# Experts and mixture of a transformer megakernel as one unrolled instruction stream, with a gate per pair of sequences

## The chip, the cores and the metric

The kernel runs on one core of a Trainium2 chip. The metric is the time on the device in microseconds (us), the median of several executions. The engines are named as in the profile: PE is TensorE, PEld its weight load, DVE is VectorE, ACT is ScalarE, POOL is GpSimd, SP is SyncE, which issues most DMAs.

## The reference, cut to what matters

Sixteen sequences of 128 tokens and 128 features go through two transformer layers. Everything before the last two steps is left as it is by the change, apart from the places named below. The last two steps are these (`_L1_cond2_ref`, then `x = x + _L1_ffn_ref(x)`):

```python
s0, s1, s2 = (_dense(x, share_wi[i], share_wo[i]) for i in range(3))   # relu(x @ wi) @ wo, hidden width 512
out_a = relu(x @ expert_wi[type_idx]) @ expert_wo[type_idx]            # one of 3 types per sequence
out_b = relu(x @ expert_wi[type_idx + 1]) @ expert_wo[type_idx + 1]
p = softmax(gate_vecs / 0.1); wa, wb = p[type, type], p[type, type + 1]
expert_out = out_a * wa + out_b * wb
gi = concatenate([expert_out[:, 0], s0[:, 0], s1[:, 0], s2[:, 0]])     # the first token alone
g = softmax(relu(gi @ gate_w1) @ gate_w2)                              # 4 numbers per sequence
x = expert_out * g[0] + s0 * g[1] + s1 * g[2] + s2 * g[3]
# mixture: every token goes to one of 8 small networks (128 -> 128 -> 128)
idx = argmax(softmax(x @ Wg + bg))
x = x + (gelu(x @ W1[idx] + b1[idx]) @ W2[idx] + b2[idx])
```

## The kernel before

Features lie on the partitions and tokens along the free axis: `XT` is 128 x 2048 (16 sequences of 128 columns), `ZT` a second such tensor. Each engine has its own program, written out by hand and ordered by semaphores; there is no scheduler. The kernel runs in stages: a causal attention, a rigid transform of images, six layers of local attention with a feed-forward part (`pe_local`, `dve_local`, `act_local`, unrolled on every engine, the last slots being the drain of the last feed-forward chunk), a gated linear attention (GLA, a loop `Fori` over 4 chunks of 4 sequences), then what the change touches.

**Gate.** `gate_pe`, `gate_dve`, `gate_act` work out the gate for all 16 sequences before the experts start. The gate needs the first token's output of every expert, so `gate_pe` multiplies the 16 first columns (`first`) by all seven experts' up weights (L1682: 28 matmuls, each two records in the trace) and down weights (L1689, 28 more), then by `gate_w1` (L1694) and `gate_w2` (L1698). `gate_dve` also works out the type weights wa and wb (L1717 to L1741), and `scale5`, five factors per sequence, at the end. A float32 matmul is two records, a transpose one.

**Experts.** `Fori(0, B // 2)` runs over pairs of sequences, ten jobs a pair, five a sequence (two chosen experts, three shared). A job n is `up`: four matmuls 128 x 128 x 128 into a bank (L1788), a relu with the gate's factor (job even: ACT, L1827; job odd: DVE, L1824), and `down`: four matmuls (L1800), which accumulate all five jobs of a sequence in one 128 x 128 area of PSUM. PE's order is up(n+1), down(n). `experts_pe` starts every pair afresh with up(0). When a sequence is done, DVE copies it to `ZT` (L1831). POOL copies the two chosen experts' weights next to each other (`e_sel`, L1843 and L1844), two sequences ahead at most.

**Mixture.** `Fori(0, NCH)` runs over 4 chunks of 512 tokens. In each, DVE copies the chunk to `m_src` (L1888), PE computes the routing logits (L1853), DVE turns them into a one-hot matrix in six small ordered steps (L1890 to L1901), PE transposes it (L1858), DVE copies it out twice (L1904, L1905). Then PE starts with the biases `m_b2` (L1862) and goes through eight experts: up (L1867) and a matmul that spreads the one-hot row over the partitions (L1868), ACT Gelu (L1918), DVE product (L1908), PE down (L1875). DVE adds the result to `XT` (L1911). All of a chunk comes after all of the one before.

**Output.** When all four chunks are done, PE transposes `XT` in four groups (L1969), DVE copies each to `ZT` (L2032) and SP stores 1 MB in one DMA (L613).

Of the kernel before, what the change touches and what calls it, by code (L numbers as in the profile page):

```python
# [60 lines left out]
E_FREE, E_DOWN = 2, 10  # L61
ME = 8

# [48 lines left out]
class Semaphores:  # L112


    def __init__(self, sem):
# [91 lines left out]
        self.e_first = sem("e_first")  # L207
        self.e_gate_made = sem("e_gate_made")
        self.e_gate_read = sem("e_gate_read")
        self.e_steps = sem("e_steps")  # L210
        self.e_arg = sem("e_arg")
        self.e_exp = sem("e_exp")
        self.e_scales = sem("e_scales")
# [5 lines left out]
        self.e_scaled = sem("e_scaled")  # L219
        self.m_loaded = sem("m_loaded")  # L220
        self.m_copied = sem("m_copied")
# [47 lines left out]
def build(nc, d, out):  # L269
    with ExitStack() as ctx:  # L270
# [145 lines left out]
        first = sb("first", [P, B])  # L416
        gate_h = xf[0][:, 0:NEXP * FJ * B]
        gate_in, gate_hid = sb("gate_in", [P, 4 * B]), sb("gate_hid", [P, B])
        gate_p, gate_max, gate_diag = sb("gate_p", [B, 4]), sb("gate_max", [B, 1]), sb("gate_diag", [B, 4 * B])
# [3 lines left out]
        pick, expw = sb("pick", [P, 4 * B]), sb("expw", [P, 4 * B])  # L423
        scale5 = sb("scale5", [P, B, 5])
        e_scale = [sb(f"e_scale{i}", [P, 5]) for i in range(2)]
        e_h = t1
        m_w1, m_w2 = wv, wo[:, :, :].rearrange("p c e -> p (c e)")
        m_pick = sb("m_pick", [ME, ME * P], BF16)
        m_b2 = sb("m_b2", [ME, P])
        m_hotT, m_hot16 = qkT[0][0:ME, :], sb("m_hot16", [ME, CW], BF16)  # L430
        m_gate, m_gate_b, m_rank = sb("m_gate", [P, ME]), sb("m_gate_b", [P, ME]), sb("m_rank", [P, ME])
        m_logits, m_hot, m_max = sb("m_logits", [P, CH * ME]), sb("m_hot", [P, CH * ME]), sb("m_max", [P, CH])
        m_src, m_g, m_h = sq[0], t2, qn
# [23 lines left out]
        def live(t):  # L457
            return 0 <= t < LOCAL

        @block.sync  # L460
        def _(sp):
# [69 lines left out]
            sp.wait_ge(s.consts_set, 4)  # L531
# [34 lines left out]
            sp.dma_start(m_b2[:, :], d["L1_ffn_b2"]).then_inc(s.m_loaded, 16)  # L566
# [3 lines left out]
            for t in range(LOCAL + 32):  # L570
# [41 lines left out]
            sp.wait_ge(s.out_ready, 4)  # L612
            sp.dma_start(out.rearrange("b t f -> t b f"), ZT[:, :].rearrange("p (b f) -> p b f", b=B))\  # L613
                .then_inc(s.out_stored, 16)
            sp.wait_ge(s.out_stored, 16)

# [438 lines left out]

        def pe_local(pe):  # L1060
# [153 lines left out]
        def dve_local(dve):  # L1214
# [58 lines left out]
            dve.wait_ge(s.consts_set, 4)  # L1273
            tables(0)
            for u in range(SLOTS):
# [68 lines left out]
                if u % TICKS == TICKS // 2 and u // TICKS + 1 < DEPTH:  # L1344
                    tables(u // TICKS + 1)
                t = u - L_SCORE
# [9 lines left out]
        def act_local(act):  # L1356
# [23 lines left out]
            for u in range(SLOTS):  # L1380
# [36 lines left out]
                if live(t) and not bursts(u):  # L1417
                    act.wait_ge(a.qkT_ready, TICKS + t + 1)
                    act.wait_ge(a.sc_ready, TICKS + t - 1)
                    act.copy(qkT[t % 2][:, :], turn_ps[:, :]).then_inc(a.qkT_moved, 1)  # L1420
                if live(u) and u % GROUPS == 0:
# [254 lines left out]
        def gate_pe(pe):  # L1676
            pe.wait_ge(s.e_loaded, 16 * 9)
            pe.wait_ge(s.e_first, 1)
            for e in range(NEXP):
                for j in range(FJ):  # L1680
                    at = (e * FJ + j) * B
                    mm = pe.matmul(bank[0][:, at:at + B], up_of(e)[:, j * P:(j + 1) * P], first[:, :],  # L1682
                                   start=True, stop=True)
            mm.then_inc(s.e_gate_made, 1)
            pe.wait_ge(s.e_gate_read, 1)
            for e in range(NEXP):
                for j in range(FJ):
                    at = (e * FJ + j) * B
                    mm = pe.matmul(bank[1][:, e * B:(e + 1) * B], down_of(e)[:, j, :], gate_h[:, at:at + B],  # L1689
                                   start=(j == 0), stop=(j == FJ - 1))  # L1690
            mm.then_inc(s.e_gate_made, 1)
            pe.wait_ge(s.e_gate_read, 3)
            for k in range(4):
                mm = pe.matmul(bank[2][:, 0:B], gw1[:, k, :], gate_in[:, k * B:(k + 1) * B], start=(k == 0),  # L1694
                               stop=(k == 3))
# [434 lines left out]
```

## Time and profile before

| | us |
|---|---|
| median of three runs (2888.82 to 2893.68) | 2891.81 |
| the profiled execution's own time | 2897.6 |
| its span in the trace | 2894.8 |
| PE busy in the span | 2542.0 (88%) |
| DVE busy | 2098.2 (72%) |
| ACT busy | 1895.1 (65%) |
| mean granted TensorE clock | 0.949 |

The span is one execution as the profiler recorded it; 2.8 us of its time lie outside the span. "Granted clock" is the share of TensorE's full clock that the chip let through: 1.00 is 2.4 GHz, 0.50 is 1.2 GHz. Times that begin with a position (2604.37) count from the start of the span.

### The profile page before, as it was taken

How to read it: one execution, taken by the hardware profiler on the slowest of the kernel's cores; microseconds unless marked ns; L12 is line 12 of the kernel's file. 1: busy time of each engine (PE TensorE's matmuls, PEld its weight loads, DVE VectorE, ACT ScalarE, POOL GpSimd, SP SyncE). 2: the span in 40 equal slices, each digit the busy share in tenths (PEclk: the TensorE clock that was granted, in tenths of full speed). 3: DMA queues.
4: the chain of work that ended last, by engine and by line, in shares of the span. 5: the costliest groups of instructions: out<-in, count | busy, mean ns of one | idle time of the engine just before them, and what ended most of it. 6: DMA issues, size and time to landing. Idle time of an engine off the chain costs nothing.

```text
span 2894.8 us, 99523 instructions
## 1 busy us (share of the span) xinstructions
PE 2542.0 (88%) x36565; PEld 1731.7 (60%) x36565; DVE 2098.2 (72%) x4476; ACT 1895.1 (65%) x6628; POOL 1778.7 (61%) x1601
## 2 busy tenths in 40 slices
PE   6999787789999999999999999999999955569987
PEld 4566544456666666666666666666666623259932
DVE  6777799978888888888888888888888734432222
ACT  3666788867888788877888888877878722221121
POOL 1666787578777777777777777777777701002100
PEclk9999999999999999999999999999999966669987
DMA  4000100021112111211121111111111100000000
GB/s 128 10 11 11 45 13 13 11 77 34 32 40 54 38 33 40 53 39 32 39 54 39 32 43 50 40 32 44 49 39 32 32 19 0 0 0 0 0 0 14
DMA packets 177362, 92.10 MB, mean 32 GB/s; under 512 B 40902, under 2 KB 173208, under 8 KB 176928
## 3 DMA queue, kind: packets, MB, share of 16 engines
q1 hardware_dynamic: 168304, 82.00, 11.0%
q0 software_dynamic: 8192, 4.21, 1.1%
q8 instruction: 276, 4.52, 0.7%
q14 instruction: 158, 1.29, 0.1%
q10 hardware_dynamic: 432, 0.07, 0.0%
HBM read 32.06 MB, written 3.76 MB: 12 GB/s over the span
## 4 chain that ended last, share of the span: by engine, by line
POOL 32%; issue 19%; PE 17%; DVE 6%; ACT 3%; DMA 1%; SPq 1%; DVEq 0%; POOLq 0%; ACTq 0%; PEld 0%; PEldq 0%
POOL rs L1463 15%; POOL t_pair L1453 11%; POOL pr L1444 5%; PE bank L1800 2%; PE bank L1788 2%; PE bank L1084 1%; PE bank L1867 1%; PE scores L1129 1%; PE bank L1140 1%; DMA rg_prod<-vt 1%; PE scores L1875 1%; PE bank L1077 1%; PE bank L1169 1%; PE scores L1111 1%; ACT pr L1392 1%
## 5 line engine op out<-in xcount | busy, mean ns | idle before, releaser
L1463 POOL TENSOR_TENSOR rs<-ssc,neg_half 128x8 f32<-128x8 f32 x384 | 645.4, 1681 | 30.1 <-DVE ssc L1343 30.1
L1453 POOL TENSOR_TENSOR t_pair<-qn_pair,tabs 128x512 f32<-128x512 f32 x384 | 489.0, 1273 | 11.4 <-DVE qn_pair L1327 9.1
L1392 ACT ACTIVATE pr<-scores,negmax 128x64 f32<-128x64 f32 x1536 | 463.4, 319 | 3.8
L1444 POOL TENSOR_TENSOR pr<-pr,rec 128x256 f32<-128x256 f32 x384 | 235.7, 614 | 340.7 <-DVE rec L1320 340.7
L1077 PE MATMUL bank<-wqk,xs 128*128 128x512 f32 x768 | 396.8, 599 | 4.7 <-DVE qn_pair L1327 3.6
L1392 ACT ACTIVATION_READ_ACCUMULATOR pr<-scores,negmax 128x1 f32 x1536 | 321.5, 209 | 0.0
L1386 ACT COPY vt<-bank 128x256 f32<-128x256 f32 x361 | 134.5, 373 | 284.9 <-PE bank L1140 244.5
L1012 POOL DMA_INDIRECT rg_win<-rg_images,share_down x256 | 260.5, 1018 | 83.3 <-issue 55.8
L1084 PEld LDWEIGHTS bank<-ident,qr_pair 128*128 128x128 f32 x1536 | 180.2, 142 | 180.3 <-DVE qr_pair L1309 141.4
L1327 DVE TENSOR_TENSOR qn_pair<-bank,rs 128x512 f32<-128x512 f32 x384 | 260.4, 678 | 19.1 <-POOL rs L1463 19.1
L1309 DVE TENSOR_TENSOR qr_pair<-t_pair 128x512 f32<-128x512 f32 x384 | 264.7, 689 | 10.0
L1140 PE MATMUL bank<-wv,xs 128*128 128x256 f32 x768 | 269.5, 433 | 0.0
L1295 DVE TENSOR_TENSOR t_pair<-qn_pair,tabc 128x512 f32<-128x512 f32 x384 | 267.6, 697 | 0.0
L1084 PE MATMUL bank<-ident,qr_pair 128*128 128x128 f32 x1536 | 238.7, 278 | 29.0 <-DVE qr_pair L1309 26.0
L1339 DVE TENSOR_REDUCE ss<-sq 128x8 f32<-128x512 f32 x384 | 261.4, 681 | 2.9 <-ACT sq L1410 2.9
L1420 ACT COPY qkT<-bank 128x512 f32<-128x512 f32 x361 | 217.4, 602 | 58.2 <-PE bank L1084 54.8
L1352 DVE TENSOR_REDUCE negmax<-scores 128x4 f32<-128x256 f32 x384 | 162.9, 424 | 124.0 <-PE scores L1129 123.6
L1410 ACT ACTIVATE sq<-bank 128x512 f32<-128x512 f32 x384 | 244.2, 636 | 8.5 <-PE bank L1077 8.4
L1094 PEld LDWEIGHTS bank<-oT,wo 128*128 128x128 f32 x1536 | 232.6, 192 | 20.5 <-issue 0.5
L1094 PE MATMUL bank<-oT,wo 128*128 128x128 f32 x1536 | 234.6, 275 | 0.0
L1066 PEld LDWEIGHTS bank<-ident,pr 128*128 128x128 f32 x768 | 108.5, 142 | 201.7 <-issue 199.4
L1129 PE MATMUL scores<-pT,vt 64*64 64x64 f32 (+1 forms) x3072 | 211.9, 231 | 10.9 <-issue 5.6
(315 smaller groups left out, 5607.6 us busy)
## 6 DMA issues: line engine op xcount, KB each, us to landing
rg_prod<-vt SPq DMA_DIRECT2D x1536, 32.0 KB
wqk<-in_L_ffn_Wqkv SPq DMA_DIRECT2D x20, 256.0 KB, 3.1
rg_win<-rg_images,share_down POOLq DMA_INDIRECT x256, 2.4
wv<-in_L_ffn_Wqkv SPq DMA_DIRECT2D x20, 128.0 KB, 2.7
wo<-in_L_ffn_Wo SPq DMA_DIRECT2D x20, 128.0 KB
w<-in_L_ffn_W SPq DMA_DIRECT2D x6, 341.0 KB
rg_images<-rg_prod SPq DMA_DIRECT2D x1, 1625.0 KB, 8.4
rg_images<-XT SPq DMA_DIRECT2D x16, 64.0 KB, 1.5
```

Source lines behind the costliest of these rows:

```text
L1012: pool.indirect_dma_start(rg_win[:, b, g, :], None, rg_images.unsqueeze(1), bass.IndirectOffsetOnAxis(rg_index[:, n:n + 1], 0)).then_inc(s ...
L1077: pe.matmul(qk_ps[t % 2][:, :], xs[b % 2][:, :], wqk[:, g, :, :].rearrange("p i n -> p (i n)"), start=True, stop=True).then_inc(a.qk_ready, 1)
L1084: mm = pe.transpose(turn_ps[:, c * P:(c + 1) * P], qr[t % 2][:, c * P:(c + 1) * P], ident[:, :])
L1094: mm = pe.matmul(yl_ps, wo[:, 2 * g + c, :], oT[b % 2][:, (2 * g + c) * P:(2 * g + c + 1) * P], start=(g == 0 and c == 0), stop=(g == GROU ...
L1140: pe.matmul(vl_ps, xs[b % 2][:, :], wv[:, g * GV:(g + 1) * GV], start=True, stop=True)\
L1295: dve.tensor_tensor(t1[t % 2][:, :].rearrange("p (i h e) -> p i h e", i=2, h=GH), qn[t % 2][:, :].rearrange("p (i h e) -> p i h e", i=2, h ...
L1309: dve.tensor_tensor(qr[t % 2][:, :], t1[t % 2][:, :], t2[t % 2][:, :], ALU.add)\
L1339: dve.tensor_reduce(ss[t % 2][:, :, 0], heads(sq[t % 2][:, :]), AX.X, ALU.add).then_inc(a.summed, 1)
L1392: ex = act.activation(pr[t % 2][:, h * BAND:(h + 1) * BAND], sl_ps[:, h // 2, h % 2 * BAND:(h % 2 + 1) * BAND], ACT.Exp, bias=negmax[t % 2 ...
L1444: pool.tensor_tensor(p, p, over(rec[t % 2][:, :], [P, GH, BAND], 2), ALU.mult).then_inc(a.p_scaled, 1)
L1453: pool.tensor_tensor(t2[t % 2][:, :].rearrange("p (i h f e) -> p i h f e", i=2, h=GH, f=2), qn[t % 2][:, :].rearrange("p (i h f e) -> p i ...
L1463: pool.tensor_tensor(rs[t % 2][:, :], ssc[t % 2][:, :], neg_half[:, 0:8], ALU.pow)\
```

## The change

1. *Gate.* The separate gate stage is gone. Instead the experts keep their outputs apart: `down` writes the two chosen experts (scaled by wa and wb in the relu) to columns 0 to 127 of a bank and each shared expert to columns of its own. One bank (2 to 5) belongs to one sequence. From the first column of each of the four parts the gate of a pair is worked out within the stream of jobs: DVE copies (`first_token`), PE multiplies (`hidden`, `logits`), DVE and ACT form the softmax (`logits`, `soften`), and DVE mixes the four parts with the four factors into `ZT` (`combine`: four operations of 128 x 128 a sequence). This happens 10 to 17 jobs after the pair's first job.
2. *Type weights.* wa and wb (`types_dve`, 14 small operations with an Exp on ACT in the middle) move to the drain of the local stage, slot `LOCAL + L_PROJ + 2`.
3. *One stream.* Experts and mixture are unrolled: 80 jobs, then 32 (`MJOBS`). Routing of chunk 0 goes inside the experts (jobs 60 to 65), that of chunk c+1 inside chunk c. `m_src` is gone, PE reads `ZT`.
4. *Selection.* POOL prepares the first two sequences' weights before GLA.
5. *Output.* Each chunk is transposed one chunk later inside the stream (`turn_out`), copied by ACT (`leave`) and stored with a DMA of its own (256 KB).
6. *Padding.* `m_pick`, `m_b2`, `m_hotT`, `m_hot16` get 128 rows instead of 8, zeroed by POOL at the start, after the local stage and after GLA.

```diff
+        def experts_pe(pe):
+            def up(n):
+                b, x = divmod(n, 5)
+                if x == 0:
+                    pe.wait_ge(s.e_chosen, 2 * b + 2)
+                if n >= 2:
+                    pe.wait_ge(s.e_relu, n - 1)
...
+            def down(n):
+                b, x = divmod(n, 5)
+                pe.wait_ge(s.e_relu, n + 1)
+                if x == 0 and b >= 4:
+                    pe.wait_ge(s.e_moved, b - 3)
...
+                part = max(x - 1, 0) * P
+                for j in range(FJ):
+                    mm = pe.matmul(bank[2 + b % 4][:, part:part + P], w[:, j, :], e_h[n % 2][:, j * P:(j + 1) * P],
+                                   start=(x != 1 and j == 0), stop=(x != 0 and j == FJ - 1))
...
+            def hidden(i):
+                pe.wait_ge(s.e_gate_read, 4 * i + 2)
+                for k in range(4):
+                    mm = pe.matmul(hid_ps, gw1[:, k, :], gate_in[:, k, :], start=(k == 0), stop=(k == 3))
+            def logits(i):
+                pe.wait_ge(s.e_gate_read, 4 * i + 3)
+                for u in range(2):
+                    mm = pe.matmul(logit_ps[:, 4 * u:4 * u + 4], gate_hid[:, u:u + 1].to_broadcast([P, P]), gw2[:, :],
...
+            up(0)
+            for n in range(JOBS):
+                if n + 1 < JOBS:
+                    up(n + 1)
+                down(n)
+                i, step = gate_at(n)
+                if step == 2:
+                    hidden(i)
+                if step == 4:
+                    logits(i)
+                if n == M_FIRST:
+                    moe_logits(pe, 0)
+                if n == M_FIRST + 4:
+                    moe_turn(pe, 0)
+            pe.wait_ge(s.m_loaded, 16 * 6)
+            hidden(PAIRS - 1)
+            moe_up(pe, 0)
+            logits(PAIRS - 1)
...
+            def combine(i):
+                dve.wait_ge(s.e_exp, i + 2)
+                ordered(dve.tensor_reduce(gate_max[:, :], gate_p[:, :, :], AX.X, ALU.add))
+                ordered(dve.reciprocal(gate_max[:, :], gate_max[:, :]))
+                ordered(dve.tensor_tensor(gate_p[:, :, :], gate_p[:, :, :], over(gate_max[:, :], [P, 2, 4], 2), ALU.mult))
+                for k in range(4):
+                    for u in range(2):
+                        b = 2 * i + u
+                        to, part, by = ZT[:, b * P:(b + 1) * P], bank[2 + b % 4][:, k * P:(k + 1) * P], gate_p[:, u, k:k + 1]
+                        if k:
+                            dve.wait_ge(s.e_mixed, 6 * i + 2 * k - 1 + u)
+                            mix = dve.scalar_tensor_tensor(to, part, by, to, ALU.mult, ALU.add)
+                        else:
+                            mix = dve.tensor_scalar(to, part, by, None, ALU.mult)
...
+            for n in range(1, JOBS, 2):
+                relu_dve(dve, n)
+                if n % 10 == 7:
+                    first_token(2 * (n // 10))
+                i, step = gate_at(n)
+                if step == 1:
+                    first_token(2 * i + 1)
+                if step == 3:
+                    hidden(i)
+                if step == 5:
+                    logits(i)
+                if step == 7:
+                    combine(i)
+                if n == M_FIRST + 1:
+                    moe_choose(dve, 0)
+                if n == M_FIRST + 5:
+                    moe_hot(dve, 0)
+            first_token(B - 1)
+            hidden(PAIRS - 1)
+            logits(PAIRS - 1)
+            combine(PAIRS - 1)
...
+            for k in range(MJOBS):
+                c, e = divmod(k, ME)
+                if k + 1 < MJOBS:
+                    moe_up(pe, k + 1)
+                down(k)
+                if e == 1 and c + 1 < NCH:
+                    moe_logits(pe, c + 1)
+                if e == 5 and c + 1 < NCH:
+                    moe_turn(pe, c + 1)
+                if e == 3 and c:
+                    turn_out(c - 1)
+            turn_out(NCH - 1)
...
+            for c in range(NCH):
+                sp.wait_ge(s.out_ready, c + 1)
+                sp.dma_start(out[CH * c:CH * (c + 1)].rearrange("b t f -> t b f"),
+                             ZT[:, c * CW:(c + 1) * CW].rearrange("p (b f) -> p b f", b=CH)).then_inc(s.out_stored, 16)
...
+                if u == LOCAL + L_PROJ + 2:
+                    act.wait_ge(s.e_arg, 1)
+                    act.activation(typew[:, :], typew[:, :], ACT.Exp).then_inc(s.e_exp, 1)
...
+            pool.wait_ge(s.e_loaded, 16 * 9)
+            for b in range(2):
+                choose(pool, b)
             with pool.Fori(0, NCH) as c:
                 gla_pool(pool, c)
```

Here `gate_at(n)` gives pair `i = (n - 10) // 10` and step `(n - 10) % 10`.

## Rows read from the trace of the kernel before

**Rows 1.** The page: the span, and POOL's busy tenths in 40 slices.

```profile
span 2894.8 us, 99523 instructions
POOL 1666787578777777777777777777777701002100
```

**Rows 2.** Busy time by stage: window, length, then PE, PEld, DVE, ACT, POOL, clock.

```profile
2573.49:2604.37 30.88, 24.44 (x124) 23.88 (x125) 7.45 (x37) 1.14 (x3) 2.28 (x3) 0.55 0.00 1
2617.38:2636.86 19.48, 18.65 (x161) 18.09 (x161) 4.65 (x9) 3.44 (x5) 4.05 (x4) 1.00 0.00 1
...
2761.65:2792.50 30.85, 26.58 (x54) 8.72 (x54) 8.63 (x18) 6.78 (x9) 0.00 (x0) 0.78 0.00 1
...
2884.95:2894.80 9.85, 2.34 (x16) 1.69 (x16) 3.26 (x5) 0.00 (x0) 0.00 (x0) 0.80 0.38 106
```

**Rows 3.** Timeline of the gate stage: start, length, engine, what, idle before.

```profile
2573.79 0.16 DVE L1717 TENSOR_REDUCE typem<-typew 128x3 f32<-128x12 f32 x1
...
2574.02 4.40 PE L1682 MATMUL bank<-first,e_up_w 128*128 128x16 f32 x32 [1.26 <-DVE first L1712]
...
2574.45 0.21 ACT L1771 ACTIVATE typew<-typew 128x12 f32<-128x12 f32 x1 [0.23 <-DVEq L1720]
...
2604.37 3.56 PE L1788 MATMUL bank<-XT,rg_win 128*128 x16 [2.49 <-POOL rg_win L1844]
```

**Rows 4.** Timeline of the experts, the break in a pair and one job.

```profile
2635.60 0.29 DVE L1831 COPY ZT<-bank 128x128 f32 x1 [3.64 <-PE bank L1800]
...
2636.86 1.15 PE L1800 MATMUL bank<-t_pair,rg_win 128*128 128x128 f32 x8 [0.51 <-DVE t_pair L1824]
...
2637.85 1.06 PE L1788 MATMUL bank<-XT,bqk 128*128 x8
...
2639.12 0.75 DVE L1824 TENSOR_SCALAR t_pair<-bank,e_scale 128x512 f32<-128x512 f32 x1 [2.39 <-PE bank L1788]
...
2640.53 1.06 PE L1800 MATMUL bank<-t_pair,share_down 128*128 128x128 f32 x8
```

**Rows 5.** Timeline of the mixture's first chunk: routing, then two experts.

```profile
2762.68 1.06 PE L1853 MATMUL bank<-m_gate,sq 128*128 128x8 f32 x8 [1.15 <-DVE sq L1888]
...
2765.14 1.02 PE L1858 MATMUL bank<-ident,m_hot 128*8 128x128 f32 x4 [1.40 <-DVE m_hot L1901]
...
2779.45 0.69 DVE L1908 TENSOR_TENSOR qn_pair<-t_pair,bank 128x512 f32<-128x512 f32 x1 [3.33 <-ACT t_pair L1918]
...
2780.86 1.12 PE L1875 MATMUL scores<-qn_pair,wo 128*128 128x512 f32 x2
...
2781.82 1.02 PE L1867 MATMUL bank<-sq,wv 128*128 128x512 f32 x2
...
2783.09 1.12 PE L1875 MATMUL scores<-qn_pair,wo 128*128 128x512 f32 x2
```

**Rows 6.** Windows of 3 us around the start of the mixture.

```profile
2764.00:2767.00 3.00, 1.02 (x4) 0.35 (x4) 1.75 (x7) 0.00 (x0) 0.00 (x0) 0.60 0.01 3
...
2776.00:2779.00 3.00, 3.00 (x5) 0.72 (x4) 0.12 (x1) 0.27 (x1) 0.00 (x0) 0.63 0.00 0
```

**Rows 7.** Local stage: a group, busy and mean ns; then timeline of POOL and DVE.

```profile
L1303 DVE TENSOR_TENSOR ZT<-bank,ZT 128x128 f32<-128x128 f32 x12 | 3.4, 285 | 0.0
...
2102.09 1.63 POOL L1463 TENSOR_TENSOR rs<-ssc,neg_half 128x8 f32<-128x8 f32 x1
...
2103.01 0.68 DVE L1295 TENSOR_TENSOR t_pair<-qn_pair,tabc 128x512 f32<-128x512 f32 x1
```

**Rows 8.** Timeline of the drain of the local stage, the last chunk's Square.

```profile
2330.29 0.63 ACT L1373 ACTIVATE rg_prod<-rg_prod 128x512 f32<-128x512 f32 x1 [2.03 <-DVE rg_prod L1234]
```

**Rows 9.** Timeline of the output; then the page's DMA issues (last number: us to landing).

```profile
2886.51 1.29 DVE L2032 COPY ZT<-bank 128x512 f32<-128x512 f32 x2 [0.82 <-PE bank L1969]
...
2889.27 0.39 SPq L613 DMA_DIRECT2D out<-ZT  x1
...
wqk<-in_L_ffn_Wqkv SPq DMA_DIRECT2D x20, 256.0 KB, 3.1
```

More of the change, by code:

```diff
@@ L1671, in gla_pool @@
                 pool.tensor_tensor(grs[j % 2][:, :], gss[j % 2][:, :], neg_half[:, 0:GLH], ALU.pow).then_inc(s.g_rms, 1)
-        def gate_pe(pe):
-            pe.wait_ge(s.e_loaded, 16 * 9)
[L1678 to L1695, printed above, removed]
-            mm.then_inc(s.e_gate_made, 1)
-            pe.wait_ge(s.e_gate_read, 4)
-            pe.matmul(bank[3][0:B, 0:4], gate_hid[:, :], gw2[:, :], start=True, stop=True).then_inc(s.e_gate_made, 1)
-            pe.wait_ge(s.e_gate_read, 5)
-            pe.matmul(bank[4][:, 0:4 * B], ones[0:B, :], gate_diag[:, :], start=True, stop=True)\
-                .then_inc(s.e_gate_made, 1)
@@ new lines, in moe_hot, with moe_dve, masked, added @@
+            dve.tensor_copy(m_hot16[c % 2][0:ME, :], spot_of(c)[0:ME, :]).then_inc(s.m_hot, 1)
+        def moe_dve(dve):
+            def masked(k):
+                dve.wait_ge(s.m_gelu, k + 1)
+                if k >= 2:
+                    dve.wait_ge(s.m_up, k + 1)
+                dve.tensor_tensor(m_h[k % 2][:, :], m_g[k % 2][:, :], bank[2 + k % 2][:, :], ALU.mult)\
+                    .then_inc(s.m_masked, 1)
+            def added(c):
+                dve.wait_ge(s.m_y, c + 1)
+                dve.tensor_tensor(XT[:, chunk(c)], XT[:, chunk(c)], y_of(c), ALU.add).then_inc(s.m_added, 1)
+            for k in range(MJOBS):
+                c, e = divmod(k, ME)
+                masked(k)
+                if e == 0 and c:
+                    added(c - 1)
+                if e == 2 and c + 1 < NCH:
+                    moe_choose(dve, c + 1)
+                if e == 6 and c + 1 < NCH:
+                    moe_hot(dve, c + 1)
+            added(NCH - 1)
@@ L1919, in moe_act, with leave @@
+        def moe_act(act):
+            def leave(c):
+                act.wait_ge(s.out_turned, c + 1)
+                act.copy(ZT[:, chunk(c)], bank[4][:, :]).then_inc(s.out_ready, 1)
+            for k in range(MJOBS):
+                c, e = divmod(k, ME)
+                act.wait_ge(s.m_up, k + 1)
+                if k >= 2:
+                    act.wait_ge(s.m_masked, k - 1)
+                act.activation(m_g[k % 2][:, :], bank[k % 2][:, :], ACT.Gelu,
                                bias=cols[:, R_MB1 + e:R_MB1 + e + 1]).then_inc(s.m_gelu, 1)
+                if e == 5 and c:
+                    leave(c - 1)
+            leave(NCH - 1)
```

398 lines of the change are left out of this document (178 added, 220 removed).

## The prediction

> **What bounds the kernel now.** I read the page first, then busy time by stage, then the chain and the timeline of the last 320 us. The span is 2894.8 us [rows 1]; the change touches what lies behind 2573.49, and little before it. The reader is to see four kinds of time there.
>
> The gate stage lasts 30.9 us, from the end of GLA to the experts' first matmul at 2604.37 [rows 2, 3]. PE is busy in 24.4 of them, but with matmuls of 16 columns that mostly load weights, at a clock of 0.55.
>
> The experts run from 2604.37 to 2761.65, 157.3 us. A pair takes 19.48 us at clock 1.00 [rows 2]. Inside it 24 records, from the start of an up at 2637.85 to that of a down at 2640.53, take 2.68 us [rows 4]: 0.1117 us a record, 1.787 us a job, 17.87 us for ten. A pair loses 1.61 us where the pipeline breaks. The reader sees one break: DVE first copies the finished sequence to `ZT` (2635.60), its relu comes late, and PE waits for it until 2636.86.
>
> The mixture takes 30.85 us a chunk, 123.3 us up to 2884.95, at a mean clock of 0.78 [rows 2]. In the steady part an expert takes 2.23 us (2780.86 to 2783.09), PE without a gap [rows 5]; eight are 17.8 us. The other 13 us are routing, in which PE mostly waits for DVE, and the half clock that follows: 0.60 at 2764 to 2767, and still only 0.63 at 2776 to 2779 [rows 6], after PE had little but small matmuls and waits.
>
> The output takes 9.85 us [rows 2].
>
> **The change, part by part.**
>
> *Gate stage.* It goes as a whole. PE's first up needs `XT` and the selected weights; POOL makes these before GLA. DVE's first operation after GLA begins at 2573.79, PE's at 2574.02 with the copy of `first` between them [rows 3]. I let PE begin at 2573.8: 2604.37 - 2573.8 = **30.6 us less**. Both start with the clock in an unknown level; before, 16 records took 3.56 us, 0.22 each, so 1.7 us were lost there [rows 3]. I count the same loss after; none would be the lower bound.
>
> *Experts.* Unrolled, the eight breaks of 1.61 go: -12.9. PE gains `hidden`, 4 matmuls or 8 records a pair, and `logits`, 2 or 4 records. Tiny matmuls cost the weight load: 8 records of 8 columns took 1.06 with their drain [rows 5], the pitch is again about 0.11. So 12 x 0.1117 = 1.35 a pair, and 7 pairs in the stream: +9.4. Routing of chunk 0 adds 8 records, 0.9, and four transposes, whose records I take at 0.12: 0.5. Together -12.9 + 9.4 + 1.4 = **-2.1**.
>
> DVE's new work is hidden only if its relus stay in time, so it has to be costed. A relu starts 0.38 after the end of its up's stream (2637.85 + 8 x 0.1117 = 2638.74, to 2639.12) and lasts 0.75; its down starts at 2640.53, so it may come 0.6 late [rows 4]. DVE has one relu in two jobs, every 3.57 us. The fullest interval is that with `combine`: relu 0.75, `first_token` 0.17, three ordered small operations, eight mixes. Small ordered operations follow each other by 0.22 (three of them between 2573.79 and Exp at 2574.45) [rows 3]: 0.66. A mix is an operation on 128 x 128 with one input in PSUM; the nearest rows are 0.285 (an addition) and 0.29 (a copy) [rows 4, 7]. The wait in it is for the mix two before, of the other sequence's neighbour, which is done. I take 0.27 to 0.30 each: 2.3. Sum 3.9, so the next relu is 0.3 late, inside its slack of 0.6: nothing. Not covered, with 0.4 a mix, the interval is 4.8 and 0.6 a pair is lost, 4 us. In the intervals with `moe_choose` (six ordered steps, 1.35) and `moe_hot` the sum stays below 3.6.
>
> Behind `combine` wait ACT's next relu (by `e_relu`) and the down of the sequence four later (by `e_moved`), three jobs away. A PE head-of-line wait for `e_gate_read` finds DVE done two jobs earlier. ACT's Exp of 0.2 is small beside its idle time: ACT is busy 3.44 of 19.48 [rows 2].
>
> *Seam.* The last pair's gate is not hidden. From the end of the last down, T: `first_token` 0.2, `hidden` starts at T + 0.26 and ends at 1.3, DVE relu to 1.5; PE meanwhile does the mixture's first up and spread (1.27) to 2.5, `logits` to 2.95, then up 1 and the biases to 5.2. DVE's maximum and subtraction end at 3.5, Exp at 3.8, `combine` at 6.65, the first product (0.69 [rows 5]) at 7.35, PE goes on at 7.4. PE is thus idle or at the gate for 1.2 + 0.45 + 2.2 = 3.9 us. ACT's Gelu, which also needs another table, is ready at 5.7, before DVE.
>
> *Mixture.* 32 experts x 2.23 = 71.4. Biases 4 x 0.96 (a down alone takes 2780.86 to 2781.82 [rows 5]) = 3.8. Inside: three routings' logits 3 x 0.9 = 2.7, three transposes 1.5, three output transposes 1.5. Sum 80.9, with the seam 84.8. For a spell of half clock after the seam I add 1: the gap is 2.2 us where the old one had six with hardly any work, and 5 is the other bound (ten microseconds at half level, as after 2767 [rows 6]). 85.8 against 123.3: **-37.5**. DVE's product may be 0.7 late by the same reading (gelu, product, then down). Routing puts 0.69 + 1.35 before the next product, in a pitch of 2.23 that PE's 0.9 of logits widens: covered. If it isn't, 1 us for each of the three chunks is lost. Addition and `leave` fall where one operation of 0.7 has room.
>
> *Output.* Before, the first copy starts 1.56 after 2884.95; then 2.7 us for the rest of the copies, and 5.5 from the issue at 2889.27 to the end [rows 2, 9]. After: 1.56, one copy 0.65, one DMA of 256 KB, which lands in 3.1 [rows 9], plus 0.4 at the end: 5.7. **-4.2**; bounds -3 and -6.
>
> *Type weights in the drain.* DVE has room there, but ACT's Exp is put before the last chunk's Square, which started at 2330.29, at once when DVE was done [rows 8]. Exp can start 0.66 after DVE begins at about 2330.3 and takes 0.21 [rows 3]: Square waits until 2331.2, **+0.9**, on the chain of the drain. DVE's rest is done before the variance arrives. Bounds 0 and 2.
>
> *POOL.* Four copies of about 1 us move to the local stage's end, where POOL waits. The memsets at the start lie in a slice with POOL busy a tenth [rows 1]: nothing; uncovered a microsecond. The padding to 128 rows doesn't change the columns that a matmul streams: nothing, and no row prices it otherwise.
>
> *A rule that speaks against it.* In rows 7 a DVE operation with two SBUF inputs starts at 2103.01, in the middle of a POOL operation of 1.63 us on SBUF that began at 2102.09, and takes its usual 0.68. By the Trainium skill (SBUF — State Buffer, "Who interferes with whom") such a pair of operations shares a port as an exclusive lock, and the later one fully blocks. This row doesn't agree. By that rule the sum would be as in rival 2.
>
> **Sum.** 0.9 - 30.6 - 2.1 - 37.5 - 4.2 = -73.5 us. The profiled execution, 2894.8 of span and 2.8 around it, was 5.8 us above the median, which is 0.2%; the difference carries over: 2891.8 - 73.5 = **2818 us**, 2.5% less.
>
> **The rivals.**
>
> 1. *The forecast, 0.66.* Own range 2812 to 2826.
> 2. *POOL's weight copies block `combine`, 0.06.* They start after job 5b - 9, for every second sequence beside `combine`. The gate's multiplication has two SBUF inputs; waiting for a copy of 1 us would make the interval 4.9, 0.7 beyond the slack, 5 us over seven pairs, and 1 in the drain: 2824. Rows 7 speak against it.
> 3. *DVE becomes the bound, 0.12.* Each mix costs 0.45 for waits between neighbours, and routing misses its room: combine interval 5.2, 1.0 a pair lost, 7 us; 3 in the mixture: 2828, up to 2840 with 0.6 a mix. For it speaks that ordered steps show 0.06 of wait each; against it, that mixes alternate between two sequences.
> 4. *Half clock inside the stream, 0.08.* The clock falls at the seam and at some gates. A microsecond of dense work costs one more at half level. At the seam 5 instead of 1, and 2 for each of three gates: 2828 to 2835. For: small matmuls lay before the fall [rows 6]. Against: 1.35 us of them stand in 19 dense ones.
> 5. *Slower, 0.03.* The same mechanism without recovery: the stream would have some 235 us of dense work, and all at half clock gives 3050. It is slower than before from 73 us of such work on, a third of the stream. The experts stayed at 1.00 with PE waiting 1.6 us in a pair [rows 2], so it is unlikely.
> 6. *More gain, 0.05.* No half clock at the start and seam, Exp hidden, shorter store: 2812 or less.
>
> The Trainium skill (TensorE: Matmul & The Clock Gate, "HAM oscillation — how this bites in real kernels") says that bursts with gaps between them fall back to the slow clock each time; by that the seam alone would cost rival 4's 5 us. Rows 6 show it for the old routing; none shows it for a gap of two microseconds.
>
> **How the numbers follow.** Cases 1, 2, 3, 4 lie between 2812 and 2840, which holds a good 8 in 10: I give **2812 to 2842**. A measurement of this kernel can tell 0.2%, some 6 us, from no change. Faster by more than that: all but case 5 and a hundredth for mixtures of mishaps, 0.96; same 0.01; slower 0.03.
>
> **What the profile after would show.** PE's first `up` about 0.3 us after GLA's last addition, at clock 1.00 soon after. A pitch of 19.2 us per pair, with no PE wait for a DVE relu after `combine`; if DVE is the bound, these waits stand in the list, and the mixes measure over 0.35. Last down of the experts at about 2730. One PE gap of 2 us at the seam, then a pitch of 21 us a chunk at clock 1.00, last down at about 2816. Three DMAs that land in the stream, and 3 to 4 us from the last issue to the end. In the drain, Square 0.9 later behind Exp. The forecast is wrong above all if granted clock falls below 1.00 in the stream, or if a relu waits for DVE.

## The result, and the profile after

The changed kernel takes 2805.89 us (median of four runs, 2802.16 to 2808.01) against 2890.39 (2888.82 to 2893.68) before (now four runs as well): ratio 0.9705, 95% interval 0.9688 to 0.9722, or 84.5 us less. The prediction said 73.5 less, 2818 us, with 2812 as its lower end: the sign was right and all parts but the mixture came near, the time lies 12 us below the forecast and 6 below the range. The profiled execution took 2806.27 us.

Two lines of the page of after, the span and the granted clock in 40 slices (to set against [rows 1]):

```profile
span 2804.4 us, 99010 instructions
PEclk8999999999999999999999999999999996768999
```

The last three slices, the last 210 us, stand at 9 or more; they hold all but the first 24 us of the experts, the seam, the mixture and the output. Busy time by stage (window, length, PE, PEld, DVE, ACT, POOL, clock, DMA share, GB/s), which answers to [rows 2]: what is left of the gate, one pair, all experts, the seam, the whole mixture with the seam, its second chunk, the output.

```profile
2569.40:2569.78 0.38, 0.00 (x1) 0.03 (x1) 0.01 (x1) 0.00 (x0) 0.32 (x1) 1.00 0.00 0
2633.49:2652.69 19.20, 19.20 (x173) 19.20 (x174) 6.76 (x21) 3.27 (x6) 4.04 (x5) 1.00 0.01 3
2569.78:2723.87 154.09, 154.09 (x1376) 153.68 (x1376) 53.44 (x161) 27.43 (x48) 28.53 (x29) 1.00 0.00 1
2723.87:2730.86 6.99, 4.59 (x22) 2.60 (x21) 3.96 (x17) 2.76 (x4) 0.00 (x0) 1.00 0.01 2
2723.87:2799.61 75.74, 72.70 (x229) 34.71 (x228) 34.05 (x74) 24.80 (x37) 0.00 (x0) 1.00 0.04 11
2746.84:2765.00 18.16, 18.16 (x60) 8.82 (x59) 8.54 (x18) 5.97 (x9) 0.00 (x0) 1.00 0.05 15
2799.61:2804.40 4.79, 0.66 (x5) 0.42 (x4) 0.69 (x1) 0.59 (x1) 0.00 (x0) 0.99 0.20 55
```

| stage | before | after | difference | predicted |
|---|---|---|---|---|
| gate | 30.9 | 0.4 | -30.5 | -30.6 |
| experts | 157.3 | 154.1 | -3.2 | -2.1 |
| mixture with the seam | 123.3 | 75.7 | -47.6 | -37.5 |
| output | 9.85 | 4.8 | -5.0 | -4.2 |
| sum behind GLA | 321.3 | 235.0 | -86.3 | -74.4 |

PE is busy in all of the experts' 154.09 us and in all of the 18.16 of a chunk of the mixture. Most of the difference to the forecast is one row: the mixture, with 10.1 of the 11.9 us.

The timeline at the start of the experts (start, length, engine, what, idle before and what ended it) answers to [rows 3]: PE's first up follows DVE's last GLA operation, and its 16 records take 2.02 us where they took 3.56.

```profile
2569.78 2.02 PE L1718 MATMUL bank<-XT,rg_win 128*128 128x128 f32 x16 [1.10 <-DVE XT L1647]
```

The timeline of the seam between experts and mixture:

```profile
2724.22 1.02 PE L1738 MATMUL scores<-gate_in,bqk 128*128 128x2 f32 x8 [0.35 <-DVE gate_in L1791]
...
2730.86 1.13 PE L1911 MATMUL scores<-qn_pair,wo 128*128 128x512 f32 x2 [2.05 <-DVE qn_pair L1975]
```

PE waits 2.05 us for DVE's product, as forecast (2.2), and goes on 7.0 us after the last down (forecast 7.4). The granted clock stays at 1.00 through it.

Now one expert of the mixture. First the timeline of before, the weight load and the matmul of the spread:

```profile
2782.77 0.09 PEld L1868 LDWEIGHTS bank<-m_hot,m_pick 8*128 8x128 bf16 x1 [0.76 <-issue]
2782.78 0.39 PE L1868 MATMUL bank<-m_hot,m_pick 8*128 8x512 bf16 x1
```

Then that of after, the spread and the records around it:

```profile
2736.58 1.02 PE L1899 MATMUL bank<-ZT,wv 128*128 128x512 f32 x2
2737.01 0.10 PEld L1900 LDWEIGHTS bank<-m_hot,m_pick 128*128 128x128 bf16 x1 [0.24 <-issue]
2737.44 0.38 PE L1900 MATMUL bank<-m_hot,m_pick 128*128 128x512 bf16 x1
2737.65 1.02 PE L1911 MATMUL scores<-qn_pair,wo 128*128 128x512 f32 x2
2738.51 1.02 PE L1899 MATMUL bank<-ZT,wv 128*128 128x512 f32 x2
```

An expert takes 2738.51 - 2736.58 = 1.93 us instead of 2.23 [rows 5]. The reader looks at the weight load. With 8 rows it begins when its matmul begins, at 2782.77: it could not run ahead. With 128 rows it begins 0.43 us earlier than the matmul, while the up before it still streams. The Trainium skill (TensorE: Matmul & The Clock Gate, "Part 2: What happens when you issue a matmul") says that a weight load is pulled ahead of running matmuls when their row groups don't conflict or when it goes to the background buffer. The load with 128 rows was; why the one with 8 was not, neither that sentence nor a run here says. The same place says that the time of a load goes by its columns and that the row count doesn't matter to it, and both rows agree: 0.09 us with 8 rows, 0.10 with 128. What the rows decide here is whether the load overlaps, which the runs below measure.

### The profile page after: what moved, and what is told of

It is laid out like the page before. It is cut to its first block, busy times and chain, and to the rows that moved or that the text cites. A ratio compares the mean times of both kernels' runs of the same rounds, so it can differ in the third digit from the quotient of the medians.

```text
span 2804.4 us, 99010 instructions
## 1 busy us (share of the span) xinstructions
PE 2481.9 (89%) x36537; PEld 1711.0 (61%) x36537; DVE 2106.7 (75%) x4543; ACT 1891.5 (67%) x6636; POOL 1780.9 (64%) x1605
## 4 chain that ended last, share of the span: by engine, by line
POOL 31%; issue 18%; PE 16%; DVE 4%; DMA 4%; ACT 3%; SPq 3%; POOLq 0%; DVEq 0%; ACTq 0%
POOL rs L1489 15%; POOL t_pair L1479 10%; POOL pr L1470 4%; DMA rg_prod<-vt 3%; SPq L576 3%; PE bank L1718 3%; PE bank L1731 3%; PE bank L1106 1%; PE bank L1162 1%; PE scores L1151 1%; PE bank L1099 1%; ACT pr L1415 1%; PE bank L1899 1%; PE scores L1133 1%; PE bank L1191 1%
## 5 line engine op out<-in xcount | busy, mean ns | idle before, releaser
L1479 POOL TENSOR_TENSOR t_pair<-qn_pair,tabs 128x512 f32<-128x512 f32 x384 | 488.5, 1272 | 12.4 <-DVE qn_pair L1348 9.8
```

What stands on the lines that cost most here:

```text
L1479: pool.tensor_tensor(t2[t % 2][:, :].rearrange("p (i h f e) -> p i h f e", i=2, h=GH, f=2), qn[t % 2][:, :].rearrange("p (i h f e) -> p i ...
```

## The experiments

The first question was where the 0.30 us per expert came from: the padding to 128 rows, the unrolled stream instead of the loop, `ZT` in place of `m_src`, or the two banks that alternate. The kernels stand in three groups, each on a chip of its own with its own runs of before. The first chip was slower as a whole (before 2949.57 us there), so medians are compared within a group and ratios between groups.

| run | median us | before on its chip | ratio to before, 95% |
|---|---|---|---|
| before_rows128 | 2932.46 | 2949.57 | 0.9945 (0.9926 to 0.9964) |
| after_rows8 | 2879.21 | the same | 0.9758 (0.9734 to 0.9782) |
| after_bias8 | 2865.43 | the same | 0.9722 (0.9697 to 0.9747) |
| after_route_between | 2883.4 | the same | 0.9773 (0.9752 to 0.9794) |
| after_again | 2811.0 | 2894.64 | 0.9704 (0.9682 to 0.9726) |
| after_spread64 | 2821.8 | the same | 0.9741 (0.9718 to 0.9763) |
| after_combine_8more | 2818.95 | the same | 0.9742 (0.9713 to 0.977) |
| after_one_store | 2811.46 | the same | 0.9706 (0.9684 to 0.9728) |
| before_spread128 | 2880.69 | 2894.88 | 0.9952 (0.9935 to 0.9969) |
| before_bias128 | 2884.69 | the same | 0.9957 (0.9938 to 0.9976) |
| after_ffn128 | 2814.34 | the same | 0.9716 (0.9697 to 0.9735) |
| after_drain_order | 2803.01, one run | the same | none |

### The padding alone, in the kernel before

```diff
-m_pick = sb("m_pick", [ME, ME * P], BF16)
+m_pick = sb("m_pick", [P, ME * P], BF16)
-m_b2 = sb("m_b2", [ME, P])
+m_b2 = sb("m_b2", [P, P])
-m_hotT, m_hot16 = qkT[0][0:ME, :], sb("m_hot16", [ME, CW], BF16)
+m_hotT, m_hot16 = qkT[0], sb("m_hot16", [P, CW], BF16)
```

POOL zeroes all four; loop, `m_src`, gate and routing stay as they were.

> The kernel before with one part of the change alone: the operands of the spread matmul and of the bias matmul have 128 rows (120 of them zero) instead of 8. Theory A (rows): a weight load of 8 rows, and the load after it, are not pulled ahead of the running matmul, which costs about 0.1 us at each switch. Then the pitch of an expert at full clock falls from 2.23 us to 1.93 or 2.0, 0.3 x 32 = about 9 us less, ratio 0.9967. Theory B (loop): the pitch fell because the mixture is unrolled; then the pitch stays 2.23 and the ratio is 1.000. Theory C (operands elsewhere, ZT in place of the copy, other PSUM banks): as B here.

The chain of before_rows128 (start, length, what), in the first chunk:

```profile
2827.99 0.22 PE bank L1868
2828.20 0.86 PE scores L1875 x2
...
2830.14 0.86 PE scores L1875 x2
```

Two downs are 1.94 apart, in the loop, with `m_src` and the banks of before. That is the whole pitch of after, so the unrolling, `ZT` and the banks are not its cause.

### The padding taken out of the changed kernel

```diff
-m_pick[:, e * P:(e + 1) * P], m_hot16[c % 2], start
+m_pick[0:8, e * P:(e + 1) * P], m_hot16[c % 2][0:8], start
-m_b2[:, :], m_hotT[:, :], start
+m_b2[0:8, :], m_hotT[0:8, :], start
```

> The changed kernel with the spread and bias matmuls reading 8 rows again. Theory A: pitch of an expert back from 1.93 to 2.23 us, about 10 us more than the changed kernel (2816, ratio to the kernel before 0.974). Theories B and C: pitch stays 1.93, ratio stays 0.9705.

The chain of after_rows8:

```profile
2804.80 0.32 PE bank L1900
2805.11 1.06 PE scores L1911 x2
...
2807.35 1.05 PE scores L1911 x2
```

The 2.23 are back. Beside the chain above it can be read where they come from: the spread holds PE for 0.32 instead of 0.22, since its own weights are loaded with nothing streaming, and the down behind it for 1.06 instead of 0.86, since its weights have to wait for the spread to finish. The ratio rises from the 0.9704 of after_again to 0.9758.

A second kernel keeps 128 rows in the spread and 8 in the biases (the last two lines of the diff alone):

> The changed kernel with only the bias matmul (one a chunk) at 8 rows. Theory A: 4 x 0.2 to 0.4 us, under 2 us in all, not to be told from 2805.9 by the median. If the cost of 8 rows lay in the bias matmul, some 10 us.

Its ratio is 0.9722, 0.0018 or 5 us above after_again; the intervals overlap, so this is read in the profile. The biases and the down behind them took 1.05 each instead of 0.86, 1.5 us over four chunks. The rest is at the seam, where the clock fell at 2780.24 and came back at 2787.07 (read in windows of 0.5 us). The window between:

```profile
2780.24:2787.07 6.83, 5.75 (x8) 2.38 (x9) 2.31 (x5) 0.91 (x2) 0.00 (x0) 0.50 0.00 0
```

PE was busy for 5.75 us at half the clock, so some 3 were lost: this is the spell that I had priced at 1 and, as a rival, at 5. It came in the two kernels with an 8-row bias matmul in the seam (after_rows8 stood at 0.50 from 2791.03 to 2797.86, as long), and in none of the eight other traces of the changed kernel and its variants, all at 1.00 there. Among these are after_spread64, whose 64-row spreads lie in the seam, and after_route_between, which ran on the same slower chip as the two. Each of these is one profiled execution; that the bias matmul is the cause is likely by the count, not shown.

### How many rows does it take

```diff
-m_pick[:, e * P:(e + 1) * P], m_hot16[c % 2], start
+m_pick[0:64, e * P:(e + 1) * P], m_hot16[c % 2][0:64], start
```

> The changed kernel with the spread matmul at 64 rows instead of 128. If any operand short of 128 rows keeps the next weight load from being pulled ahead, the pitch is 2.23 us and the time some 10 us more. If only very few rows do (8), the pitch stays 1.93.

The chain of after_spread64:

```profile
2747.41 0.32 PE bank L1900
2747.73 1.06 PE scores L1911 x2
```

Sixty-four rows cost what eight cost, 0.32 and 1.06, and the pitch is again 2.23; the median is 10.8 us above after_again's, for 32 x 0.30 = 9.6. So the time does not follow the number of rows; what is lost is lost at the switch to these rows and back. But not any number short of 128 loses it. The local stage has a float32 pair with 85 rows between two groups with 128. The timeline of after there:

```profile
1040.07 0.30 PEld L1209 LDWEIGHTS bank<-rg_prod,w 85*128 85x128 f32 x2
1040.18 1.02 PE L1209 MATMUL bank<-rg_prod,w 85*128 85x512 f32 x2
1041.04 0.60 PE L1106 MATMUL bank<-ident,qr_pair 128*128 128x128 f32 x4
```

Its weights are loaded 0.11 before it starts, while the transposes ahead of it still run, and the next group starts 0.86 behind its start, as behind a pair with 128 rows. It is so in all 22 such places before the drain (0.86 or 0.87). With 8 and 64 rows the overlap is lost, with 85 it is not; between 64 and 85 nothing was tried.

### Spread and biases apart, in the kernel before

Before_rows128 had gained 0.0055 of 2890, 16 us, where the pitch gives 9.6. Two kernels pad one operand each: before_spread128 `m_pick` and `m_hot16`, before_bias128 `m_b2` and `m_hotT`.

> The kernel before with only the spread matmul (eight a chunk) at 128 rows, the bias matmul at 8. By the theory of rows: pitch 1.93, 9 us less. The kernel with both at 128 rows gained 16 us, because the clock also came back about 4 us after the routing instead of 10. If the spread matmuls do that too, the whole 16 us (ratio 0.9945) are here; if it is the bias matmul, 9 us (0.997).

> The kernel before with only the bias matmul (one a chunk, the first after the routing) at 128 rows, the spread at 8. Pitch 2.23. If the bias matmul brings the clock back earlier, its chunk is some 2 us shorter, 6 to 8 us in all (0.9975); if not, no difference.

A chunk of before takes 30.85. The distances of the biases' starts in the chains are 26.6, 26.9, 27.1 with the spread padded, 28.4, 28.0, 27.9 with the biases, 26.6, 26.3, 25.6 with both. The pitch explains 2.4 of it for the spread and nothing of this size for the biases. The rest is clock. The table gives, for the four chunks of each kernel, how long the clock stood at half (read in windows of 0.5 us), and when it came back, counted from the start of the biases:

| kernel | at half clock, us | back after the biases' start, us |
|---|---|---|
| before | 13.7, 13.7, 13.7, 13.7 | 10.7, 10.4, 10.3, 10.2 |
| before_spread128 | 6.8, 10.2, 10.2, 10.2 | 5.8, 6.6, 6.9, 7.1 |
| before_bias128 | 6.8, 6.8, 6.8, 6.8 | 5.8, 4.7, 4.1, 3.5 |
| before_rows128 | 6.8, 10.2, 6.8, 6.8 | 4.8, 5.5, 3.1, 4.8 |

Before_rows128 ran on the slower chip. The windows of before in its first chunk, of before_spread128 in its second and of before_bias128 in its first, each from the fall to the return:

```profile
2764.58:2778.24 13.66, 11.73 (x16) 3.23 (x16) 3.09 (x7) 1.37 (x2) 0.00 (x0) 0.50 0.00 1
```

```profile
2788.15:2798.39 10.24, 7.58 (x13) 2.80 (x14) 3.03 (x9) 0.69 (x1) 0.00 (x0) 0.50 0.00 0
```

```profile
2765.73:2772.56 6.83, 5.82 (x7) 1.78 (x7) 1.64 (x3) 0.69 (x1) 0.00 (x0) 0.50 0.00 0
```

From the biases' start to the return PE is busy almost without a gap in all four kernels. Either padding alone brings the clock back sooner: the one bias matmul a chunk halves the time at half clock, the eight spread matmuls take 3.4 to 6.8 us off it, and both together take no more off than the biases alone. So full rows bought two things: the pitch, and an earlier return of the clock. The medians can't rank the three (their intervals overlap); the distances in the chains, one execution of each, can: 3.7 to 4.3 us a chunk gained with the spread, 2.5 to 3.0 with the biases, 4.2 to 5.2 with both. The medians fell by 14.2 (9 or 16 expected) and 10.2 (6 to 8 expected). What in the 8-row matmuls delays the clock the windows don't show.

### Routing between the chunks

```diff
-                if k + 1 < MJOBS:
+                if e < ME - 1:
                     moe_up(pe, k + 1)
                 down(k)
-                if e == 1 and c + 1 < NCH:
-                    moe_logits(pe, c + 1)
-                if e == 5 and c + 1 < NCH:
-                    moe_turn(pe, c + 1)
+                if e == ME - 1 and c + 1 < NCH:
+                    moe_logits(pe, c + 1)
+                    moe_turn(pe, c + 1)
+                    moe_up(pe, k + 1)
```

DVE's `moe_choose` and `moe_hot` move to the same place.

> The changed kernel with the routing of chunks 1 to 3 between the chunks again, nothing else changed. It prices the overlap. If the wait itself is the whole price: logits, six steps, transposes, two copies, product chain, about 7 us a chunk, of which about 1.3 are work that PE does anyway: 3 x 5.5 = 17 us more. If the clock falls as in the kernel before, another 4 to 5 a chunk: 30 us more.

The ratio is 0.9773 against 0.9704, some 20 us for three chunks. One window of after_route_between over a chunk's start, and the timeline inside it:

```profile
2804.28:2813.20 8.92, 6.01 (x19) 2.87 (x19) 3.36 (x10) 0.69 (x1) 0.00 (x0) 0.62 0.00 0
```

```profile
2809.00 2.08 PE L1899 MATMUL bank<-ZT,wv 128*128 128x512 f32 x2 [1.44 <-DVE rg_win L1968]
```

PE idles 2.9 of 8.9 us while DVE routes, in two waits of 1.47 and 1.44, and the clock is down: two records of up take 2.08 instead of 1.02. It stood at half for 6.8 us at the first of the three breaks and for 3.4 at the other two. The seam, with one wait of 2.05, kept its clock, these breaks didn't; routing inside the chunk is worth both the waits and the clock. The 20 us lie near the branch of the expectation without a fall of the clock (17), though the clock did fall: the 30 of the other branch were too many.

### Eight more operations in `combine`

```diff
+                if i < PAIRS - 1:
+                    for _ in range(8):
+                        ordered(dve.tensor_copy(e_idle[:, :], ident[:, :]))
```

The copies are extra work that nobody reads; the computation stays whole.

> The changed kernel with eight additional ordered copies of 128 x 128 on DVE behind the mixes of each pair but the last (unused result). Theory of the prediction: the next relu has 0.6 us of slack and DVE is just done in time, so of 8 x 0.25 = 2.0 us added, 1.4 a pair come through on PE, 7 x 1.4 = 10 us more in all, and the waits stand at the down after the relu behind combine. If DVE had no slack at all: 14 us. If DVE was not near the bound: nothing.

The timeline of after from the relu before `combine` to the one behind it, with six of the eight mixes:

```profile
2601.91 0.69 DVE L1778 TENSOR_SCALAR t_pair<-bank 128x512 f32<-128x512 f32 x1 [2.42 <-PE bank L1718]
...
2603.70 1.63 DVE L1815 SCALAR_TENSOR_TENSOR ZT<-bank,gate_p,ZT 128x128 f32<-128x128 f32 x6
2605.49 0.69 DVE L1778 TENSOR_SCALAR t_pair<-bank 128x512 f32<-128x512 f32 x1 [0.15 <-PE bank L1718]
```

Relu to relu is 3.58, one interval of two jobs, and DVE is idle for 0.15 in it: the relu, `first_token` and `combine` take 3.4 together, of which the six mixes are 1.63, 0.27 each, where I had 3.9 and 0.27 to 0.30. The same spot of after_combine_8more, then its list of waits (us, times, longest):

```profile
2605.24 2.17 DVE L1822 COPY e_idle<-ident 128x128 f32<-128x128 f32 x8
2607.44 0.69 DVE L1779 TENSOR_SCALAR t_pair<-bank 128x512 f32<-128x512 f32 x1
2608.19 1.16 PE L1732 MATMUL bank<-t_pair,share_down 128*128 128x128 f32 x8 [0.96 <-DVE t_pair L1779]
```

```profile
PE bank L1732 <- DVE t_pair L1779: 7.5, 7, 1.7
```

The relu comes 1.95 late and the down 1.12: the slack behind `combine` is 0.8 us, and beyond it DVE sets the pace. Seven waits of 7.5 us in all, where the expectation had 10; the median rose by 8.0. Rival 3 was thus near: with DVE's 0.15 of idle time, 0.12 us more in each of the eight mixes would have used up the slack.

### One store instead of four

```diff
-            for c in range(NCH):
-                sp.wait_ge(s.out_ready, c + 1)
...
+            sp.wait_ge(s.out_ready, 4)
+            sp.dma_start(out.rearrange("b t f -> t b f"), ZT[:, :].rearrange("p (b f) -> p b f", b=B))
```

> The changed kernel with one store of 1 MB at the end instead of four by chunk. Theory: the last store then moves 1 MB behind the last copy, 5.5 us from issue to the end as in the kernel before instead of about 3: 2.5 us more, 0.1%, which the profile shows and the median hardly.

From the end of ACT's last copy to the end of the span are 5.5 us with one store (2804.73 to 2810.2) and 2.7 with four (in after_again 2813.59 to 2816.3), so the small stores take 2.8 off the tail in the profile. The medians, 2811.46 and 2811.0, don't tell the two apart.

### The same padding in the local stage

The feed-forward part of the local stage has a third down matmul over 85 rows (`w2[0:w, j, :]`, `hg[j][0:w, :]`, w = 85). The kernel gives it 128, with the rest of both operands zeroed at the start.

> The changed kernel with the third down matmul of the local feed-forward part (24 in all, 85 rows) at 128 rows, the rest zero. By the theory of rows each switch costs 0.1 us, two to four a matmul: 5 to 10 us less if PE bounds that stage, ratio 0.968. If POOL's chain bounds it, as the chain of waits says with its 31%, nothing: 0.9705.

Ratio 0.9716 against 0.9704: no gain. In the 200 us from 1000 on PE is busy 190.75 in after and 190.73 here. The expectation offered two reasons, and the trace of after gives a third: the matmuls with 85 rows lost nothing to begin with, since their weights were loaded ahead (the rows at 1040.18 above). So this kernel does not test whether the padding would pay in a stage that PE doesn't fill.

### Exp and POOL's copies in the drain

The kernel puts ACT's Exp behind the last Square and lets POOL copy the first weights only when GLA begins:

```diff
                 c, step = ffn_step(u)
                 if c is not None:
                     ffn(c, step)
+                if u == LOCAL + L_PROJ + 2:
+                    act.wait_ge(s.e_arg, 1)
+                    act.activation(typew[:, :], typew[:, :], ACT.Exp).then_inc(s.e_exp, 1)
...
             pool.wait_ge(s.e_loaded, 16 * 9)
+            pool.wait_ge(s.x_final, NCH)
             for b in range(2):
```

> The changed kernel with Exp on ACT behind the last chunk's Square and POOL's four copies moved to GLA's first chunk; a look at the profile, since the time can't show it. Square should start about 0.05 us after DVE is done, as in the kernel before, instead of 0.7. If POOL's copies had blocked DVE, the scale and shift operation on 128 x 512 in the drain takes 0.55 us again instead of 0.79, and operations with two SBUF inputs at the start of GLA get longer than 0.69 instead.

The timeline of after in the drain, then at GLA's start:

```profile
2326.71 0.69 DVE L1256 TENSOR_TENSOR rg_prod<-xf,bank 128x512 f32<-128x512 f32 x1 [1.28 <-PE bank L1171]
2327.98 0.21 ACT L1446 ACTIVATE typew<-typew 128x12 f32<-128x12 f32 x1 [2.58 <-DVEq L1067]
2328.10 0.61 ACT L1396 ACTIVATE rg_prod<-rg_prod 128x512 f32<-128x512 f32 x1
...
2330.48 0.16 DVE L1261 TENSOR_SCALAR xv<-bank 128x4 f32<-128x4 f32 x1
...
2333.13 1.03 POOL L1867 COPY rg_win<-rg_win 128x1024 f32 x1
2333.65 0.79 DVE L1269 TENSOR_SCALAR rg_prod<-rg_prod,cols 128x512 f32<-128x512 f32 x1
...
2361.52 0.17 DVE L1575 TENSOR_SCALAR xf<-XT 128x8 f32 x1
```

And that of after_drain_order:

```profile
2322.55 0.63 ACT L1396 ACTIVATE rg_prod<-rg_prod 128x512 f32<-128x512 f32 x1 [2.04 <-DVE rg_prod L1256]
...
2325.35 0.20 DVE L1079 TENSOR_REDUCE type_scale<-pick 128x16 f32<-128x48 f32 x1
2325.59 0.16 DVE L1261 TENSOR_SCALAR xv<-bank 128x4 f32<-128x4 f32 x1
...
2328.77 0.55 DVE L1269 TENSOR_SCALAR rg_prod<-rg_prod,cols 128x512 f32<-128x512 f32 x1
...
2355.43 1.15 POOL L1866 COPY rg_win<-e_up_w 128x1024 f32 x1 [28.12 <-DVE XT L2086]
2355.60 1.01 DVE L1575 TENSOR_SCALAR xf<-XT 128x8 f32 x1
2356.53 1.30 POOL L1867 COPY rg_win<-rg_win 128x1024 f32 x1
2356.97 1.41 DVE L1579 SCALAR_TENSOR_TENSOR xf<-XT,xf 128x512 f32<-128x512 f32 x1
2357.77 1.50 POOL L1866 COPY rg_win<-e_up_w 128x1024 f32 x1
```

In after, Square starts 0.7 us behind the end of DVE's addition, because Exp came first; in after_drain_order it follows DVE at once. It gains nothing by it: the step that reads the variance, which POOL starts behind DVE's L1261, begins 4.01 us after the addition began in after and 4.00 in after_drain_order (3.47 in before). What L1261 waits for in both is DVE itself, which ends the type weights (L1079) only then; in after_drain_order PE's sums were ready at 2325.10, DVE at 2325.55. The move of Exp is worth nothing as long as DVE has these to do first.

The copies do matter. In after DVE's scaling meets them and takes 0.79 instead of 0.55. In after_drain_order they lie beside GLA's first operations instead. There an operation on 8 columns takes 1.01 us instead of 0.17 and ends at 2356.61, where POOL's copy ends (2356.58); the next with two SBUF inputs takes 1.41 instead of 0.69 and ends 0.55 behind the second copy; the copies take up to 1.50 instead of 1.04. These ends fit one engine standing while the other works; at half speed an operation of 0.17 would not take 1.01. From DVE's additions to `XT` (L2086) to the first projection on PE (L1503) pass 12.4 us instead of 9.5. The two moves together lose some 2.6 us in the trace; one run at 2803.01 can't show that.

None of the twelve kernels beats the changed one by a measurable amount.

## Why the prediction was right and where it was wrong

**Bound and gate stage: right.** The stage went, -30.5 against -30.6, and PE's first up came 0.38 behind GLA.

**Experts: right in mechanism.** The pitch of a pair is 19.20, as forecast. The eight breaks are gone and the gate's records lie in the stream. The 1.1 us more came from the clock: I counted the 1.7 us loss of [rows 3] again, and the first 16 records ran at 1.00 and took 2.02, 1.5 less. The 0.4 the other way I can't assign.

**DVE's slack: right.** No relu came late; the mixes took 0.27, and the slack of 0.8 us (shown by eight more copies) held. I had called the next relu 0.3 late; it was not late at all. POOL's copies in the stream (rival 2) made no PE wait.

**Seam: right.** 7.0 against 7.4, one wait of 2.05. The 1 us for a spell at half clock was not needed: the clock stayed. This may hang on the padding, since with an 8-row bias matmul it fell in both traces. After_bias8, with 3 us lost, came nearest to rival 4. The section of the Trainium skill that I held against the forecast (TensorE: Matmul & The Clock Gate, "HAM oscillation — how this bites in real kernels") has waits in its example that are longer than the seam's 2.05 us, so a seam at 1.00 neither bears it out nor contradicts it.

**Mixture: wrong, this is the step that failed.** The prediction says that "the padding to 128 rows doesn't change the columns that a matmul streams: nothing, and no row prices it otherwise", and it takes 2.23 us an expert over from [rows 5]. A row did price it: the four float32 records of an expert take 0.43 each and the spread 0.22, 1.93 in all, and 2.23 stood in the chain. 0.30 us were therefore not streaming, though PE was listed as busy, and I did not ask what they were. They were weight loads that could not run ahead, one for the spread and one for the down behind it, at each change between 8 and 128 rows. The sum by terms: 32 x 0.30 = 9.6, biases 0.4 in all, the clock at the seam 1.0, logits and transposes 0.7 (0.79 and 0.44 each instead of 0.9 and 0.5), less 0.64 of a wait for the last product: 11.1, against the 10.1 that the stages show. About a microsecond the other way I can't assign. The 0.4 by which the seam was shorter don't count again: its spreads and biases are in the terms above. A chunk took 18.16 instead of the 21 that I gave.

**The rivals.** The time fell where rival 6 had put it, at 2812 or less, but not by its reasons. The clock at the start and at the seam gave 1.5 and 1.0, the output 0.8 more than forecast, and the drain about nothing: some 3 of the 12 us. No rival held the 9.6 of the mixture.

**Output: right.** -5.0, between the bounds: ACT's copy took 0.59, and 2.7 us from its end instead of 3.5 to the end.

**Drain: near in the number, by luck; wrong in the wait.** I said that Square waits 0.9 for Exp and that "DVE's rest is done before the variance arrives". Square waited 0.7, but after_drain_order shows that this wait was not the last: without it the variance step came just as late, 0.54 behind before, because DVE was still at the type weights. Another 0.24 came from a POOL copy in DVE's way. Together 0.8.

**POOL and DVE: a rule set aside too early.** I read [rows 7] as saying that such pairs don't hinder each other. After_drain_order shows that a pair of this kind does: the row was of a POOL operation with eight columns, here it is a copy of 1024. Which property of the two makes the difference wasn't tried. The Trainium skill (SBUF — State Buffer, "Who interferes with whom") names this pair, two SBUF inputs on DVE against POOL reading SBUF, as an exclusive lock, and says that the later one is fully blocked. The rows of after_drain_order agree: the operation on 8 columns took 1.01 us and ended with POOL's copy, and the three after it that took 1.27 to 1.41 each ended 0.54 or 0.55 behind the end of a copy. Only the POOL operation of [rows 7] doesn't fit. In the changed kernel only DVE's scaling in the drain met a copy, at 0.24; in the stream the copies lie beside the mixes (a copy starts at 2603.49, the mixes run on to 2605.33), which have one input in PSUM and kept their 0.27.

**The carried difference.** Of the 90.4 us between the spans 4.1 lie ahead of the change's part (GLA ends at 2573.49 and 2569.40); the medians differ by 84.5, near the 86.3 behind GLA less the drain's wait.

## What to carry to other kernels

When PE is listed as busy without a gap, add up what its records must take and hold it against the pitch: a remainder of 0.1 to 0.3 us at each matmul with few rows (8 and 64 here) is a weight load that isn't hidden, and zero rows up to 128 removed it at no measured cost. Look first whether the load really starts late: with 85 rows it didn't, and padding bought nothing. And before you conclude from a row that a DVE and a POOL operation don't disturb each other, look whether it shows operations of the sizes that you will have. When a wait looks like the price of a change, move it away and see whether the next step comes earlier; in the drain it did not.

## What the runs showed of the hardware that was not expected

- A matmul with 8 or 64 rows between such with 128 costs 0.3 us: 0.1 for its own weights and 0.2 for those behind it. 8 and 64 rows cost the same; 85 rows cost nothing (0.86 us for the pair, load 0.11 ahead).
- With 128 rows in the biases, one matmul a chunk, the clock stood at half for 6.8 us after the routing instead of 13.7, in all four chunks; with 128 rows in the spread alone for 6.8 to 10.2 (one trace each). A break of 2 us at the seam left it at 1.00 in eight traces, and it fell in the two with an 8-row bias matmul there.
- DVE and a large POOL copy, both reading SBUF, took turns at the start of GLA in after_drain_order: 0.17 became 1.01 us, 0.69 became 1.27 and 1.41, the copies 1.15 to 1.50 where others take 1.04. A POOL operation with eight columns left DVE's 0.68 alone [rows 7].
